# Upper halves of an expert tile's rows transposed by DMA, lower halves by TensorE

## The reference

```python
x = x + tanh(g_xattn) * xattn(layernorm(x), ctx_768, ...)
y = layernorm(x)
gate_weights = softmax(einsum('bsd,de->bse', y, gate_w) + gate_b)
topk_values, topk_indices = top_k(gate_weights, 2)
hidden = relu(einsum('bsd,edh->bseh', y, w1) + b1)
expert_out = einsum('bseh,ehd->bsed', hidden, w2) + b2
x = x + tanh(g_ffn) * sum_over_the_2_chosen(topk_value * expert_out)
```

## Time and profile before

| | |
|---|---|
| median of three executions | 634.6 us |
| the profiled execution | 638.39 us, span 636.7 us |
| mean granted PE clock | 0.880 of full speed |
| PE busy | 520.9 us (82%), 4723 matmuls |
| DVE, ACT, POOL busy | 404.2, 415.4, 271.8 us |
| HBM read, written | 33.19 MB, 24.49 MB |

### The profile page before, as it was taken

The page is one execution under the profiler, slowest core; times in us unless marked ns, Lnnn a source line. Parts: engine busy times, 40 slices in busy tenths (PEclk is TensorE's granted clock), DMA queues, the critical chain, the costliest instruction groups (busy, mean ns, idle before and its releaser), DMA issues.

```text
span 636.7 us, 15679 instructions
## 1 busy us (share of the span) xinstructions
PE 520.9 (82%) x4723; PEld 430.4 (68%) x4724; DVE 404.2 (63%) x1157; ACT 415.4 (65%) x1061; POOL 271.8 (43%) x288
## 2 busy tenths in 40 slices
PE   6958417508778999987799999877999999999991
PEld 2537206306467887765588877756989999999991
DVE  3268799588376676873466677745755565665650
ACT  2387874656346776754466766646888788888880
POOL 3110228513583223966523238665476622233331
PEclk9585555557799999997899999979999999999997
DMA  6919505824432324134322332333333333333221
GB/s 172 328 39 379 178 0 186 282 71 124 151 86 52 43 36 109 28 79 94 69 44 35 44 83 55 69 85 87 54 72 58 53 53 52 52 53 51 36 27 17
DMA packets 47634, 57.07 MB, mean 90 GB/s; under 512 B 6856, under 2 KB 43198, under 8 KB 47424
## 3 DMA queue, kind: packets, MB, share of 16 engines
q1 hardware_dynamic: 32223, 36.60, 18.7%
q0 software_dynamic: 14064, 18.55, 17.0%
q10 hardware_dynamic: 1264, 0.93, 0.5%
HBM read 33.19 MB, written 24.49 MB: 91 GB/s over the span
## 4 chain that ended last, share of the span: by engine, by line
PE 50%; DVE 18%; issue 12%; ACT 11%; DMA 4%; ACTq 1%; POOL 1%; another core or an unknown queue 1%; DVEq 1%; SPq 0%; POOLq 0%
PE hid L1730 8%; PE hid L1734 7%; PE bank L1754 6%; PE bank L1752 6%; PE bank L1753 6%; PE hid L1731 4%; PE hid L1733 4%; ACT pool L866 4%; DVE pool L1407 3%; DVE w1l L957 2%; DVE w2l L957 2%; PE bank L1711 2%; ACT w2l L727 2%; DMA out_dram<-pool,idx 2%; PE bank L1593 2%
## 5 line engine op out<-in xcount | busy, mean ns | idle before, releaser
L659 POOL DMA_INDIRECT out_dram<-pool,idx x71 | 114.8, 1617 | 229.2 <-DVE pool L1422 186.3
L866 ACT ACTIVATE pool<-hid,b1s 128x128 f32<-128x128 f32 x568 | 166.7, 374 | 53.1 <-remote 29.6
L1730 PE MATMUL hid<-pool,w1h 128*128 128x256 f16 x568 | 158.8, 280 | 8.8 <-DVE pool L1407 5.0
L1752 PE MATMUL bank<-w2h,pool 128*128 x568 | 154.9, 273 | 10.3 <-issue 9.8
L1407 DVE TENSOR_TENSOR pool<-hid,pool 128x512 f32<-128x512 f32 x142 | 96.8, 690 | 101.5 <-ACT pool L866 87.3
L1734 PE MATMUL hid<-pool,w1h 128*128 128x256 f16 x568 | 158.9, 280 | 2.1 <-issue 2.1
L1753 PE MATMUL bank<-w2l,pool 128*128 x568 | 154.8, 273 | 3.1 <-issue 3.1
L1754 PE MATMUL bank<-w2h,pool 128*128 x568 | 154.9, 273 | 0.8 <-issue 0.7
L1731 PE MATMUL hid<-pool,w1l 128*128 128x128 f16 x568 | 126.8, 223 | 2.1 <-issue 2.1
L1733 PE MATMUL hid<-pool,w1l 128*128 128x128 f16 x568 | 127.0, 224 | 1.9 <-issue 1.9
L875 ACT ACTIVATE pool<-pool 128x512 f16<-128x512 f32 x142 | 89.9, 636 | 34.4 <-DVE pool L1407 34.1
(11 more groups left out here) (257 smaller groups left out, 734.8 us busy)
## 6 DMA issues: line engine op xcount, KB each, us to landing
pool<-in_L_ffn_w_dram SPq DMA_DIRECT2D x12, 1024.0 KB
pool<-xs SPq DMA_DIRECT2D x71, 132.5 KB
xb<-in_x_dram SPq DMA_DIRECT2D x4, 1024.0 KB
out_dram<-xb SPq DMA_DIRECT2D x4, 1024.0 KB, 4.9
out_dram<-pool,idx POOLq DMA_INDIRECT x71
w1h<-in_L_ffn_w_dram SPq DMA_DIRECT2D x1, 1024.0 KB, 4.9
w1l<-in_L_ffn_w_dram SPq DMA_DIRECT2D x1, 1024.0 KB, 7.5
w2h<-in_L_ffn_w_dram SPq DMA_DIRECT2D x1, 1024.0 KB, 9.6
```

Source lines behind the costliest of these rows:

```text
L659: g.indirect_dma_start(out=out_rows, out_offset=bass.IndirectOffsetOnAxis(ap=idx[s % U][:, 0:1], axis=0), in_=y2[s % 3], in_offset=None, c ...
L866: a.activation(hb[:, c * P:(c + 1) * P], bank[c // 2][:, (2 * (c % 2) + 1) * P:2 * (c % 2 + 1) * P], ACT.Identity, bias=b1s[:, ds(e * NH + ...
L1730: t.matmul(o, wh, xhl, start=True, stop=False)
L1752: t.matmul(o, hh[s % 2][:, hs], wh, start=c == 0, stop=False)
```

## The change

`xs` is also viewed as f16 (`xs16`). Of a tile's rows, SP now loads only words 128 to 264 (lower parts, gates, token number) as they are, and issues two DMA transposes, one for each chunk of 128 features, that read the upper parts from `xs` and write them transposed straight into `xTh`. PE transposes the two lower pieces only, and ACT copies 256 instead of 512 columns, into every second 128 columns of `xTh`. `xTh` has four buffers instead of two, so the SP load of tile s now also waits until `hidden(s - 4)` is done (`g_mm1`), and `rows_T(s)` waits for `hidden(s - 4)` instead of `hidden(s - 2)`. `hidden(s)` waits for the two transposes of its tile (`g_xh`) besides ACT's copy. The buffers take the same 1572 words a partition as before.

```diff
+    xs16 = xs.bitcast(F16)
+    XL = D // 2
...
-        xg = [carve(XW) for _ in range(U)]
-        xTh = [carve(2 * ND * P, F16) for _ in range(2)]
+        xTh = [carve(2 * ND * P, F16).rearrange("p (c k t) -> p c k t", c=ND, k=2) for _ in range(U)]
+        xg = [carve(XW - XL) for _ in range(U)]
...
-        turned_x = bank[5][:, 0:ND * P].bitcast(F16)
+        turned_x = bank[5][:, 0:ND * P // 2].bitcast(F16)
...
                 if s >= U:
                     sp.wait_ge(g_T, s - U + 1)
+                    sp.wait_ge(g_mm1, NHB * (s - U + 1))
...
-                sp.dma_start(xg[s % U], xs[ds(row, P), :]).then_inc(g_xg[s % U], 16)
+                sp.dma_start(xg[s % U], xs[ds(row, P), XL:XW]).then_inc(g_xg[s % U], 16)
+                for c in range(ND):
+                    sp.dma_start(xTh[s % U][:, c, 0, :], xs16[ds(row, P), c * P:(c + 1) * P],
+                                 transpose=True).then_inc(g_xh[s % U], 16)
...
             def rows_T(s):
                 act.wait_ge(g_T, s + 1)
-                if s >= 2:
-                    act.wait_ge(g_mm1, NHB * (s - 1))
-                a.copy(xTh[s % 2], turned_x).then_inc(g_xT, 1)
+                if s >= U:
+                    act.wait_ge(g_mm1, NHB * (s - U + 1))
+                a.copy(xTh[s % U][:, :, 1, :], turned_x.rearrange("p (c t) -> p c t", c=ND)).then_inc(g_xT, 1)
...
                 for c in range(ND):
-                    for k in range(2):
-                        mm = t.transpose(o[:, (2 * c + k) * P:(2 * c + k + 1) * P],
-                                         x16[:, k * D + c * P:k * D + (c + 1) * P], ident16[:])
+                    mm = t.transpose(turned_x[:, c * P:(c + 1) * P], x16[:, c * P:(c + 1) * P], ident16[:])
                 mm.then_inc(g_T, 1)
 
             def hidden(s):
                 pe.wait_ge(g_xT, s + 1)
-                xt = xTh[s % 2]
+                pe.wait_ge(g_xh[s % U], (s // U + 1) * ND * 16)
+                xt = xTh[s % U].rearrange("p c k t -> p (c k t)")
```

More of the change, by code:

```diff
@@ L382, in gated_attention_and_routed_experts @@
         g_xg = [sem(f"g_xg{u}") for u in range(U)]
+        g_xh = [sem(f"g_xh{u}") for u in range(U)]
         def tile_tokens(ap, b):
@@ L650, in index @@
                     pool.wait_ge(g_out, (s - U + 1) * 16)
-                g.tensor_copy(idx[s % U][:], xg[s % U][:, TC:XW].bitcast(I32)).then_inc(g_ix, 1)
+                g.tensor_copy(idx[s % U][:], xg[s % U][:, TC - XL:XW - XL].bitcast(I32)).then_inc(g_ix, 1)
             def scatter(s):
@@ L1399, in gate @@
                 dve.wait_ge(g_xg[s % U], (s // U + 1) * 16)
-                v.tensor_tensor(q[s % U][:], xg[s % U][:, ds(e + GC, 1)].to_broadcast([P, 2]), inv[:, ds(2 * e, 2)], ALU.mult).then_inc(g_q, 1)
+                v.tensor_tensor(q[s % U][:], xg[s % U][:, ds(e + GC - XL, 1)].to_broadcast([P, 2]), inv[:, ds(2 * e, 2)], ALU.mult).then_inc(g_q, 1)
             def h_sum(s):
@@ L1706, in turn_rows @@
                     pe.wait_ge(g_xT, s)
-                o = turned_x
-                x16 = xg[s % U][:, 0:D].bitcast(F16)
+                x16 = xg[s % U][:, 0:XL].bitcast(F16)
                 for c in range(ND):
-                    for k in range(2):
-                        mm = t.transpose(o[:, (2 * c + k) * P:(2 * c + k + 1) * P],
-                                         x16[:, k * D + c * P:k * D + (c + 1) * P], ident16[:])
+                    mm = t.transpose(turned_x[:, c * P:(c + 1) * P], x16[:, c * P:(c + 1) * P], ident16[:])
                 mm.then_inc(g_T, 1)
```

## The result

| | before | after |
|---|---|---|
| median of 4 executions each, us | 636.09 (632.09 to 639.15) | 641.70 (640.67 to 644.99) |
| profiled execution, us | 638.39, span 636.7 | 642.68, span 641.0 |
| mean granted clock | 0.880 | 0.879 |

The ratio of after to before is 1.0104, with a 95% interval of [1.0057, 1.0151]: about 6.6 us slower, between 3.6 and 9.6, at the edge of what was called 1% slower. The forecast of 636.7 was +2.1 us on its median, which lies outside that interval. The forecast's sign and its main cost were right; its main gain was not.

The account below looks back on a forecast made before the run. It took PE to bound its busy slices, with waits at POOL's scatters and for `b2s` at the tile loop's start; -5.7 (PE) + 6.3 (`b2s`) + 1.5 (scatter stretches) = +2.1 us on 634.6 gave 636.7, range 628 to 655.

Parts of the forecast that it names:

- `b2s`, +6.3: Start of the tile loop: eight transposes on SP's queue delay the `b2s` load, and so DVE's line 1217, by 6.3 us.
- t: On SP's queue: the time one DMA transpose holds it, taken as 1.25 us, between 0.34 and 2.2.
- 8t - 3.75: Start of the tile loop: the `b2s` load's delay, eight transposes' hold of SP less its 3.75 us to spare.
- PE, -5.7: PE-bound slices, 52 tiles: two transposes fewer gain 0.11 us a tile, 5.7 us in all.
- ACT, 0: ACT's copy: 0.22 us a tile shorter, counted 0, since PE does not wait for ACT in the bound windows.
- Moved waits, 0: SP's row loads waiting for `hidden(s - 4)`: 11 us of cover are left for the transposes, so cost 0.
- Scatter stretches, +1.5: Three stretches where POOL scatters rows: added load on the DMA engines costs 0.5 us each, 1.5 in all.
- B, cheap issue: SP's queue at the start: transposes under 0.47 us fit its spare time, only the gain is left, 628.9 us; chance 0.15.
- C, SP held long: SP's queue: from 1.8 us a transpose over 1% slower, from 2.1 SP sets the late tiles' pace; chance 0.12.
- D, contention on the output scatters' chain: Late tiles: transposes and POOL's output scatters delay each other's landing, costing 14 us (about 650) to 52; chance 0.26.
- "Slower": Whole kernel: over 1% (6.3 us) slower, the chances of C and D together; chance 0.38.
- A: The forecast case: transpose hold 0.9 to 1.6 us, `b2s` delay 3.4 to 9.1, little contention, 632 to 640 us; chance 0.47.

Follow-up runs that it names:

- kernel 4: kernel 3 with the DMA transposes and SP's wait for `g_mm1` back, their results read by nobody and not waited for by PE; 1.0118 of before.
- kernel 3: The changed kernel without DMA transposes and the waits for them, matmuls reading the lower parts twice; 0.9989 of before.
- kernel 2: The kernel before, without DMA transposes, with the load of `b2s` put behind tile 4's row load; 1.0064 of before.
- kernel 8: The changed kernel with DVE's wait for `b2s` moved to its first use, `y_sum(0)`; 1.0005 of before.
- kernel 1: The changed kernel with the load of `b2s` put ahead of tile 2's loads, behind four DMA transposes instead of eight; 1.0035 of before.
- kernel 6: kernel 3 with fixed weight addresses and no register loads on PE; 0.9822 of before, late tiles 5.37 to 5.38 us apart.
- kernel 7: The kernel before, four PE transposes, with fixed weight addresses and no register loads on PE; 0.9959 of before, late tiles 5.474 us.
- kernel 5: The kernel before with six PE transposes a tile instead of four; 1.0050 of before.
- kernel 10: The kernel before with ACT's load of the expert's number taken out and a fixed bias column; 1.0009 of before.
- kernel 11: kernel 3 with ACT's load of the expert's number taken out and a fixed bias column; 0.9895 of before.
- kernel 9: The changed kernel with both `b2s` repairs, the load behind tile 1 and DVE's wait at first use; 1.0005 of before.
- kernel 12: kernel 9 with the two address loads of `output` issued ahead of groups 1 and 5 instead of 2 and 7; 1.0161 of before.

## Why the prediction was right or wrong

**`b2s`, +6.3: right in mechanism and place, in part by luck in size.** At t = 1.14 the formula 8t - 3.75 gives 5.4, but the load stood 7.8 us behind the splitting. SP took 156.81 - 141.40 = 15.4 us for the four rounds, where the formula has 3.90 + 8 x 1.14 = 13.0: one row load took 1.07 us, and the third round 153.82 - 148.97 = 4.9. The t that was taken, 1.25, was a pick between 0.34 and 2.2 and made up for a part of it. The delay cost 6.5 us at tile 4 of the changed kernel (of kernel 4, with the same wait of DVE, 4.1 against kernel 3), and kernels 2 and 8 show the mechanism, kernel 1 less sharply. The forecast place of line 1217's wait, and POOL's scatters behind it, was right. By the page of the Trainium skill that the forecast cited (VectorE: DVE Perf Modes, "The three transpose paths"), 1309 ns a transpose, it would have been 6.7. The trace has 1.14 us for SP's hold of the queue, which the page does not separate.

**PE, -5.7: wrong, and the step that failed.** "The slices at 9 tenths hold 52 tiles, so the gain is 52 x 0.11". The size of 0.11 was right (559.66 - 559.55), but the step took a busy PE for a limit that falls one for one. In the 32 late tiles the array was the limit, but the address loads on PE's sequencer lay just 0.03 us below it at the mean (kernels 3, 6, 7): 0.03 came, 0.08 did not. In the 20 tiles with attention the array was not the limit, though 98% busy: two more transposes cost 0.03 us at most (kernel 5), two fewer gave 0.03 (kernel 3), and what ended last was a copy by ACT, which showed 5.4 of 20 us free (kernels 10 and 11). So 52 x 0.03 = 1.6 us was to be had; timed without the DMA transposes it is 0.7 (kernel 3). The forecast's own sign of this, that the late tiles' period doesn't fall, came true but for the 0.03. It also counted 20 busy slices where the earlier trace rows has 21; the one left out, from 16 to 32 us, lies ahead of the tile loop, so its 52 tiles stand.

**ACT, 0: right as a sum, wrong as a reason.** The copy went from 574 ns to 362 in the changed kernel's groups by line (busy us, mean ns, idle before):

```profile
L863 ACT COPY pool<-bank 128x256 f16<-128x256 f16 x71 | 25.7, 362 | 5.5 <-PE bank L1716 3.6 <-remote 1.7
```

The forecast said 354 and that ACT isn't waited for. It is, in the attention tiles: without ACT's load kernel 3's fall from 7.02 to 6.85 us (kernel 11).

**Moved waits, 0: right.** Two views of the waits of the changed kernel, SP's queue, then PE's largest from 170 us on (us in total, times, longest):

```profile
SPq L501 <- PE hid L1739: 89.0, 43, 3.6
```

```profile
PE hid L1735 <- issue: 7.9, 14, 1.1
PE bank L1757 <- issue: 6.9, 11, 1.7
PE hid L1735 <- DVE pool L1414: 5.0, 8, 1.0
```

SP does wait for `g_mm1`, 43 times, but nobody behind it is late: from 170 us on PE has no wait for a DMA of `xs` in the view. And kernel 4, without PE's wait for `g_xh`, is no faster than the changed one (1.0118 and 1.0104).

**Scatter stretches, +1.5: neither shown nor refuted.** It was never timed by itself. The changed kernel is 7.3 us slower than kernel 3 by the ratios; less the 6.3 that kernel 8 gave back, 1.0 is left. For kernel 4 what is left beside the start and the late tiles is 3.5. Both remainders carry an uncertainty of their own size or more. With the first the sum reads -0.7 + 6.3 + 1.0 = +6.6, where the forecast had -5.7 + 6.3 + 1.5; that it closes is no proof, since the last term is what was missing.

**The rivals.** B, cheap issue: no, t is 1.14 us, more than three times an ordinary load's 0.34. C, SP held long: no. A late tile's loads hold SP from 541.72 to 544.59 us, 2.9 of 5.45:

```profile
541.72 0.34 SPq L505 DMA_DIRECT2D pool<-xs  x1
542.20 2.39 SPq L507 DMA_TRANSPOSE pool<-xs  x2
```

D, contention on the output scatters' chain: no. The forecast's sign was whether the output scatters wait for DVE or for their own DMA. The view of POOL's waits from 480 to 605 us of the changed kernel (us in total, times, longest):

```profile
POOL out_dram L666 <- DVE pool L1429: 59.4, 16, 3.9
...
POOL out_dram L666 <- DMA out_dram<-pool,idx: 1.0, 1, 1.0
```

In the same tiles of before they wait 59.1 us for DVE and 1.3 for the DMA, so the chain did not become the limit. "Slower" thus came true, if only just, by none of the mechanisms that its 0.38 stood for, but by A with a smaller gain; that the range of 628 to 655 holds the 641.7 measured is owed in part to room that was left for C and D. What was missing is the rival "PE's gain is held up by the next limit", in the size of 4 to 5 us.

## What to carry to other kernels

An engine that is 100% busy is worth speeding up only down to its next limit. Look for that one first, its own sequencer included: the time of its register loads in a period against the period. The quick test is to lengthen the work by as much as you mean to save, and to leave it out without paying for it (kernels 5 and 3 here), before the replacement is built. And where a queue gets slower instructions, ask which of the loads behind them somebody waits for, and whether that wait stands earlier than the first use: moving it cost nothing that shows here and returned 6.3 us.

## What the runs showed of the hardware that was not expected

**A DMA transpose is dear for the queue, cheap for the DMA engines.** The DMA queues in 440 to 620 us (packets, MB, share of 16 engines), of the changed kernel, then of kernel 3:

```profile
q0 software_dynamic: 5520, 5.15, 22.0%
q1 hardware_dynamic: 13920, 4.08, 12.1%
```

```profile
q1 hardware_dynamic: 4320, 2.11, 5.1%
```

The 60 transposes of 128 x 128 f16 in that window take 7.0% of 180 us, 0.21 us of all engines each, in 9600 / 60 = 160 packets; the forecast had 0.14, the plain load's rate, to 1.2. Each holds SP's queue for 1.14 us (0.84 to 2.12).

**Loading 16 registers takes PE's sequencer 1.28 us** at the median, three times a tile, and at times over 2 (2.48 in tile 11 of before). The array stood idle behind such loads for 0.10 us of a late tile with two transposes, and for 1.5 us of tile 11.

**The chip matters more than the change.** The kernel before took 636.27 and 639.43 us at the median on two chips (kernels 1 to 8), and 610.20 and 609.96 on two others (kernels 9 to 12). On one of those tiles 13 to 19 of kernel 10 take 37.15 us and tiles 27 to 37 65.15, where the first profile of before has 51.63 and 76.89; the late tiles take 5.50 there and 5.49 here. Tiles 19 to 27 take 62.04 there against 55.06, so a part is lost again. The difference is in the stretches with POOL's scatters, and the granted clock differs there too: 0.83 from 280 to 300 us of before, 1.00 from 250 to 290 us of kernel 10, where its tiles 13 to 19 lie. What makes it stays open, and ratios are to be taken on one chip only.
